# Resampling stage: x1 is added on TensorE, the bias in the last sum, and the first offsets of a window are made a step earlier

## What is computed

```
x1  = x  + dilation(groupnorm(x))                  # morphological dilation, 11 x 11 taps
out = x1 + deformable(groupnorm(x1))
# deformable(v): h = depthwise3x3(proj(v)); h = gelu(batchnorm(h))
#   offset = tanh(off_w @ h) * 1/255               # 2 channels: dy, dx for each pixel
#   bilinear sampling of v at (pixel + 0.5 + offset), zero outside the image
```

```
ph  = (tx + 1) * dh
f   = 0.5 * (tx + 1) * dd + dv
out = ph + (ty + 1) * f + scale * x1 + bias
```

## Time and profile before

| what | value |
|---|---|
| median of 3 runs | 11159.03 us (11152.15 to 11159.74) |
| the profiled execution: its time, its span | 11149.29 us, 11147.4 us |
| `resample`, first to last DVE instruction of its loop | from 10161.93 to 11143.07 us of the span |
| busy share of the whole span | DVE 95%, ACT 89%, POOL 82%, PE 75% |
| TensorE's granted clock, mean of the span | 0.922 |

### The profile page before, as it was taken

How to read it: one execution, slowest core, us unless ns; L and a number is a source line. 1 busy time by engine, 2 the same in 40 slices (tenths; PEclk the granted TensorE clock), 3 DMA queues, 4 the chain that set the end, 5 groups by cost and what they waited for, 6 DMA issues and landing times. The chain is left out here.

```text
span 11147.4 us, 74869 instructions
## 1 busy us (share of the span) xinstructions
PE 8347.9 (75%) x16532; PEld 3201.8 (29%) x16532; DVE 10631.9 (95%) x5882; ACT 9898.5 (89%) x7193; POOL 9104.7 (82%) x2891
## 2 busy tenths in 40 slices
PE   1777777777777777777777777777777777886665
PEld 0222222222222222222222222222222223332222
DVE  8999999999999999999999999999999998998999
ACT  2999999999999999999999999999999987776666
POOL 2888888888888888888888888888888885666777
PEclk9999999999999999999999999999999998998888
DMA  7666666666666666666666666666666663444555
GB/s 286 128 128 129 129 129 129 129 128 128 128 128 128 129 125 126 128 128 128 125 129 127 129 125 128 127 128 126 129 128 128 126 120 157 159 160 168 212 213 213
DMA packets 386979, 1573.30 MB, mean 141 GB/s; under 512 B 20944, under 2 KB 127568, under 8 KB 324432
## 3 DMA queue, kind: packets, MB, share of 16 engines
q0 software_dynamic: 218256, 901.04, 44.9%
q1 hardware_dynamic: 168256, 667.25, 16.0%
HBM read 465.90 MB, written 201.33 MB: 60 GB/s over the span
## 5 line engine op out<-in xcount | busy, mean ns | idle before, releaser
L446 POOL TENSOR_TENSOR m_pool<-r_pool,u 128x2048 f32<-128x2048 f32 x1536 | 6777.4, 4539 | 919.6 <-ACT r_pool L540 860.6
L495 PE MATMUL chain<-dx,mats 128*128 128x512 f32 x6144 | 3111.2, 649 | 952.9 <-ACT chain L558 951.9
L643 DVE SCALAR_TENSOR_TENSOR acc_a<-m_pool,kt,acc_a 128x2048 f32<-128x2048 f32 x1472 | 3465.7, 2354 | 60.2 <-POOL m_pool L446 17.7
L495 PE MATMUL chain<-dx,neg_ident 128*128 128x512 f32 x4608 | 2417.7, 672 | 851.0 <-ACT chain L558 850.6
L643 DVE SCALAR_TENSOR_TENSOR acc_a<-u,kt,acc_a 128x2048 f32<-128x2048 f32 x960 | 2261.2, 2355 | 31.9
L540 ACT ACTIVATE r_pool<-dx,gap_l 128x2048 f32<-128x2048 f32 x1024 | 2051.6, 2004 | 75.4 <-POOL m_pool L446 36.2
L495 PEld LDWEIGHTS chain<-dx,mats 128*128 128x128 f32 x6144 | 1167.2, 201 | 2896.7 <-ACT chain L558 1747.4
L643 DVE SCALAR_TENSOR_TENSOR acc_a<-t,kt,acc_a 128x2048 f32<-128x2048 f32 x768 | 1808.2, 2354 | 22.8
L558 ACT ACTIVATE chain<-chain,gap_r 128x1024 f32<-128x1024 f32 x1536 | 1631.0, 1089 | 110.6 <-PE chain L495 110.2
L495 PE MATMUL chain<-u,mats 128*128 128x512 f32 x3072 | 1457.9, 606 | 216.9 <-ACT chain L558 216.9
L495 PEld LDWEIGHTS chain<-dx,neg_ident 128*128 128x128 f32 x4608 | 919.5, 211 | 2348.8 <-ACT chain L558 1458.5
(11 more groups left out here) (144 smaller groups left out, 6976.5 us busy)
## 6 DMA issues: line engine op xcount, KB each, us to landing
t<-u POOLq DMA_DIRECT2D x768, 1059.0 KB, 8.7
u<-x_dram SPq DMA_DIRECT2D x28, 3328.0 KB, 27.5
xw<-x_scratch SPq DMA_DIRECT2D x64, 1152.0 KB, 6.9
hw<-h_scratch SPq DMA_DIRECT2D x66, 1024.0 KB, 8.9
x<-xc POOLq DMA_DIRECT2D x65, 1024.0 KB, 8.8
xt<-x_dram SPq DMA_DIRECT2D x32, 2048.0 KB, 14.4
xc<-x_dram SPq DMA_DIRECT2D x64, 1024.0 KB, 4.7
x_scratch<-x SPq DMA_DIRECT2D x64, 1024.0 KB, 9.8
```

The source lines that it names most:

```text
L446: nc.gpsimd.tensor_tensor(m_pool[j % MP][:], r_pool[j % RP][:], u[s][:, k * CR + di:k * CR + di + CR, base:base + W], ALU.add).then_inc(m_ ...
L495: added = nc.tensor.matmul(chain[h][:, r:r + 2, :], weight, src[:, top:top + 2, dj:dj + W], start=False, stop=True, skip_group_check=True)
L643: nc.vector.scalar_tensor_tensor(out=acc_a[:], in0=src, scalar=k_base, in1=acc_a[:], op0=ALU.subtract, op1=ALU.max).then_inc(a_done, 1)
```

## The change

DVE has five instructions for a part instead of six. The sum `res = ph + z` is gone, and ACT makes no `z`. In its place PE multiplies `xw` by a diagonal matrix `zdiag` that holds the scale of x1 (one for each group, made once ahead of the loop), and adds the product in PSUM onto `ph`, which DVE has written there (`add_z`, two matmuls for each part). The bias is the scalar operand (`tab[:, 5, ...]`) of the last instruction, `res = (ph + bias) + f`. For the accumulation PE opens `ph` once with two matmuls ahead of the loop.

The product `(ty + 1) * f` is written into `f` in SBUF rather than into `ty`, so that `ty` is free after this instruction (`w_ready`), and no longer only after the last sum. PE issues the offsets in another order: `tx` of the second part and of the next window's first part are issued ahead of that part's `ty`, and `ge` of the next window is waited for in the middle of a window. ACT takes the tanh of the next window's first `tx` ahead of `y`. POOL's `dh` waits for `f` of window n - 2 instead of its last sum. Each DVE instruction of a part now waits for the one before it. `xw` has four buffers instead of two, and x1 is loaded three windows ahead; SP's list is written out instead of looped. The computation of `dd` from columns of `dv` is as before.

```diff
@@ -1003,7 +1003,8 @@
-    channel_mean, same_image = mats[:, 2, :], mats[:, 3, :]
+    XS = 4
+    ident, channel_mean, same_image = mats[:, 0, :], mats[:, 2, :], mats[:, 3, :]
...
+        xw = [sb(f"xw{s}", [P, VR + 1, W]) for s in range(XS)]
-        z = [sb(f"z{s}", [P, VR, W]) for s in range(2)]
...
+        zdiag = sb("zdiag", [P, GROUPS, P])
...
+        F0, W0, OFFY0, D0, R0 = 3, 1, 2, 6, 1
...
+                for n in range(NALL):
+                    g, w = divmod(n, NV)
+                    if n > 0:
+
+                        sp.wait_ge(z_added, 2 * n)
+                    load_x(n + XS - 1)
+                    sp.wait_ge(ge_ready, n + 1)
+                    load_h(n + 2)
+                    sp.wait_ge(res_ready, R0 + 2 * n + 2)
+                    sp.dma_start(out_pl[g * P:(g + 1) * P, w * (VR * W):(w + 1) * (VR * W)],
+                                 res[n % 2][:].rearrange("p r w -> p (r w)")).then_inc(stored[n % 2], 16)
...
+                def offset_x(n, s, p):
+
+                    pe.wait_ge(f_ready, n * 2 + (p - 1 + F0))
+                    for r in range(0, PR, 2):
+                        last = nc.tensor.matmul(tx[p][:, r:r + 2, :], off[:, 1, :],
+                                                ge[s % 2][:, p * PR + r:p * PR + r + 2, :], start=True, stop=True)
+                    last.then_inc(off_x, 1)
+
+                def offset_y(n, s, p):
+
+                    pe.wait_ge(w_ready, n * 2 + (p + W0))
+                    for r in range(0, PR, 2):
+                        last = nc.tensor.matmul(ty[:, r:r + 2, :], off[:, 0, :],
+                                                ge[s % 2][:, p * PR + r:p * PR + r + 2, :], start=True, stop=True)
+                    last.then_inc(off_y, 1)
+
+                def add_z(n, g, s, p):
+
+                    pe.wait_ge(o_ready, n * 2 + (p + 1))
+                    for r in range(0, PR, 2):
+                        last = nc.tensor.matmul(ph[:, r:r + 2, :], zdiag[:, g, :],
+                                                xw[s % XS][:, p * PR + r:p * PR + r + 2, :],
+                                                start=False, stop=True, skip_group_check=True)
+                    last.then_inc(z_added, 1)
...
-                with nc.Fori(0, NALL // 2, engines=PE_ONLY) as i:
-                    for s in range(2):
-                        n = i * 2 + s
-                        pe.wait_ge(ge_ready, n + 1)
-                        for p in range(2):
-
-                            pe.wait_ge(part_x, n * 2 + (p + 1))
-                            for r in range(0, PR, 2):
-                                last = nc.tensor.matmul(tx[p][:, r:r + 2, :], off[:, 1, :],
-                                                        ge[s][:, p * PR + r:p * PR + r + 2, :],
-                                                        start=True, stop=True)
-                            last.then_inc(off_x, 1)
-                            pe.wait_ge(part_y, n * 2 + (p + 3))
-                            for r in range(0, PR, 2):
-                                last = nc.tensor.matmul(ty[:, r:r + 2, :], off[:, 0, :],
-                                                        ge[s][:, p * PR + r:p * PR + r + 2, :],
-                                                        start=True, stop=True)
-                            last.then_inc(off_y, 1)
+                pe.wait_ge(ge_ready, 1)
+
+                for r in range(0, PR, 2):
+                    opened = nc.tensor.matmul(ph[:, r:r + 2, :], ident, ge[0][:, r:r + 2, :],
+                                              start=True, stop=True, skip_group_check=True)
+                opened.then_inc(ph_open, 1)
+                offset_x(0, 0, 0)
+                offset_y(0, 0, 0)
+                for g in range(GROUPS):
+                    with nc.Fori(0, NV // XS, engines=PE_ONLY) as i:
+                        for s in range(XS):
+                            n = i * XS + (g * NV + s)
+                            offset_x(n, s, 1)
+                            add_z(n, g, s, 0)
+                            offset_y(n, s, 1)
+                            pe.wait_ge(ge_ready, n + 2)
+                            offset_x(n + 1, s + 1, 0)
+                            add_z(n, g, s, 1)
+                            offset_y(n + 1, s + 1, 0)
...
+                    act.wait_ge(xw_loaded[s % XS], loads * 16)
+                    act.wait_ge(diffs, n * 3 + (D0 - 3))
...
+                    act.wait_ge(off_y, n * 2 + (OFFY0 - 2))
+                    nc.scalar.activation(ge[s % 2][:], hw[s % 2][:], ACT.Gelu, bias=bn[:, 3:4], scale=bn[:, 2:3]) \
                         .then_inc(ge_ready, 1)
-
-                def make_z(n, s):
-                    act.wait_ge(part_y, n * 2 + 1)
-                    passed(act, act_turns)
-                    nc.scalar.activation(z[s][:], xw[s][:, 0:VR, :], ACT.Identity,
-                                         bias=tab[:, 5, bass.ds(n, 1)],
-                                         scale=tab[:, 4, bass.ds(n, 1)]).then_inc(z_ready, 1)
...
-                    act.wait_ge(off_y, n * 2 + (p + 1 + 4))
+                    act.wait_ge(off_y, n * 2 + (p + 1 + OFFY0))
...
+                act.wait_ge(hw_loaded[0], 16)
+                nc.scalar.activation(ge[0][:], hw[0][:], ACT.Gelu, bias=bn[:, 3:4], scale=bn[:, 2:3]) \
+                    .then_inc(ge_ready, 1)
                 make_y(1, 1, 1)
-                make_ge(0, 0, 1)
-                make_z(0, 0)
-                with nc.Fori(0, NALL // 2, engines=ACT_ONLY) as i:
-                    for s in range(2):
-                        n = i * 2 + s
-                        make_tanh_x(n, 0)
+                make_tanh_x(0, 0)
+                with nc.Fori(0, NALL // XS, engines=ACT_ONLY) as i:
+                    for s in range(XS):
+                        n = i * XS + s
                         make_tanh_y(n, 0)
                         make_tanh_x(n, 1)
-                        make_z(n + 1, 1 - s)
-                        make_ge(n + 1, 1 - s, i + (1 + s))
+                        make_ge(n + 1, s + 1, i * 2 + ((s + 1) // 2 + 1))
                         make_tanh_y(n, 1)
-                        make_y(n + 2, s, i + 2)
+                        make_tanh_x(n + 1, 0)
+                        make_y(n + 2, s + 2, i + ((s + 2) // XS + 1))
...
-                        pool.wait_ge(part_y, n * 2 + 1)
+
+                        pool.wait_ge(f_ready, n * 2 + (F0 - 2))
...
+                    link(nc.vector.tensor_scalar(zdiag[:, g, :], ident, tab[:, 4, lo:lo + 1], None, ALU.mult))
...
-                dve.sem_inc(part_x, 2)
-                dve.sem_inc(part_y, 3)
-                dve.sem_inc(off_y, 4)
+                dve.sem_inc(f_ready, F0)
+                dve.sem_inc(w_ready, W0)
+                dve.sem_inc(off_y, OFFY0)
+                dve.sem_inc(res_ready, R0)
                 nc.vector.memset(cm[:], 0.0).then_inc(tables_ready, 1)
+                dve.wait_ge(ph_open, 1)
...
-                            at = n * 8 + 4 * p
                             rows = slice(p * PR, (p + 1) * PR)
                             part = n * 2 + (p + 1)
                             if p == 0:
-                                dve.wait_ge(stored[s], i * 16 + 16)
-                                dve.wait_ge(z_ready, n + 1)
-                                dve.wait_ge(diffs, n * 3 + 9)
+                                dve.wait_ge(diffs, n * 3 + (D0 + 3))
                             dve.wait_ge(tanh_x, part)
+
+                            dve.wait_ge(res_ready, n * 2 + (p + R0))
                             nc.vector.scalar_tensor_tensor(out=ph[:], in0=tx[p][:], scalar=1.0, in1=dh[s][:, rows, :],
-                                                           op0=ALU.add, op1=ALU.mult).then_inc(chain, 1)
+                                                           op0=ALU.add, op1=ALU.mult).then_inc(o_ready, 1)
+                            dve.wait_ge(o_ready, part)
                             nc.vector.scalar_tensor_tensor(out=tx[p][:], in0=tx[p][:], scalar=1.0,
                                                            in1=dd[s][:, rows, :],
-                                                           op0=ALU.add, op1=ALU.mult).then_inc(chain, 1)
-                            dve.wait_ge(chain, at + 1)
-                            nc.vector.tensor_tensor(res[s][:, rows, :], ph[:], z[s][:, rows, :], ALU.add) \
-                                .then_inc(chain, 1)
-                            dve.wait_ge(chain, at + 2)
+                                                           op0=ALU.add, op1=ALU.mult).then_inc(x_scaled, 1)
+                            dve.wait_ge(x_scaled, part)
                             nc.vector.scalar_tensor_tensor(out=f[:], in0=tx[p][:], scalar=0.5,
                                                            in1=dv[s][:, rows, 0:W],
-                                                           op0=ALU.mult, op1=ALU.add).then_inc(part_x, 1)
```

(17 more changed lines are left out.)

77 lines of the change are left out of this document (32 added, 45 removed).

## The result

The changed kernel takes 11005.88 us, the median of 4 runs (11004.33 to 11008.32). The kernel before, timed beside it, takes 11159.39 us (4 runs, 11152.15 to 11160.56). The ratio is 0.9865, with a 95% interval of 0.9849 to 0.9881: 1.35% faster, 153.5 us. The forecast was 10995 us, with a range of 10972 to 11065 and, for its first case, of 10975 to 11010.

The account below looks back on a forecast made before the run. DVE's chain of dependent steps was taken to bound the last stage's loop: 64 x 12.76 = 816.6 us instead of 981.1, plus 0.6 for `zdiag`, so 163.9 less: 10995 us, range 10972 to 11065.

Parts of the forecast that it names:

- first case: In the last stage's loop DVE's chain bounds, as forecast: 10975 to 11010 us in all, chance 0.70.
- DVE's chain bounds: In the last stage's loop, five DVE instructions a part, each waiting for its predecessor, set the time; chance 0.70.
- The sum of the chain: DVE's start-to-start distances in the loop: 6.33 us a part, 12.76 a window with 0.10 added, 816.6 for 64 windows.
- the distance from the last sum to the next `ph`: On DVE, put at 1.31 us after a convolution step with like operands; bounds 1.25 and 1.32.
- The 0.10 us ahead of the last sum: In a window's first part, a sequencer row waiting ahead of DVE's last sum adds 0.10 us, as in the convolution.
- The clock: PE at full speed throughout the loop, its only gap some 1.0 us a part; rival of PE bounding, slower: chance 0.05.
- The slacks: Work beside DVE's chain stays hidden: `add_z` 0.9 us early, POOL idle 0.9 a window, DMA 254 GB/s, ACT near 68%.
- The prologue: Ahead of the loop, making `zdiag` adds two small DVE instructions, 2 x 0.29 = 0.6 us.
- What the profile was to show: Loop signs: DVE 96% or more, `ph` 12.7 to 12.8 us apart, PEclk 0.97 or more, no DVE wait for POOL.
- The total: Whole kernel: 981.1 - 816.6 - 0.6 = 163.9 us less, giving 10995 us on the median.

Follow-up runs that it names:

- a1_swap: Changed kernel with the two waits ahead of DVE's `ph` in the other order, the one for the last sum first; 10999.59 us.
- a2_static_bias: Changed kernel with DVE's loop run once per channel group, so the last sum's scalar has a fixed address and needs no register; 10997.14 us.
- a3_both: Changed kernel with both the edits of a1_swap and a2_static_bias; 10993.42 us, ratio to the kernel before 0.9853.
- a4_free_tx: Changed kernel without the wait of DVE's `tx` step for the `ph` step; 10993.67 us, ratio to the kernel before 0.9852.
- c2_all_small: Changed kernel with the edits of a1_swap, a2_static_bias and a4_free_tx together; 10971.08 us, ratio to the kernel before 0.9835.
- b5_ty_early_psum: Kernel before, with the product written to `f`, `ty` released right after it, and the sum with `z` kept in PSUM; 11096.38 us, ratio 0.9947.
- b3: Changed kernel with one more product with a weight of zeros in each `add_z` group on PE; 11001.26 us.
- b4: Changed kernel with two more products with a weight of zeros in each `add_z` group on PE; 11053.93 us.
- b1_ty_early: Kernel before, with the product written to `f`, `ty` released after it, and a last sum reading two SBUF tiles; 11211.75 us, ratio 1.0051.
- b2: Changed kernel with PE's offsets and ACT's first tanh in the old order, none a step ahead; 11005.06 us, ratio to the kernel before 0.9864.
- c1_interleaved: Changed kernel with DVE's steps interleaved over two parts, none waiting for its predecessor, and earlier loads; 10931.80 us, ratio to the kernel before 0.9798.

## Why the prediction was right

**DVE's chain bounds: right, and shown.** No wait for another engine stands in a window, and every edit of the chain came out in the loop at its size: 64 windows less 0.14, 0.12, 0.26, 0.27 and 0.53 us in a1_swap, a2_static_bias, a3_both, a4_free_tx and c2_all_small.

**The sum of the chain: 12.76 forecast, 13.00 measured.** The term that was too small is the distance from the last sum to the next `ph`, put at 1.31 us: it is 1.39, and 0.08 x 128 = 10 us of the loop are this. a1_swap shows the cause, the order of two waits. Another 0.02 us a window stand before the last sum (1.38 where 1.36 was counted). The rest is about 0.01 us in most steps: they were put at 1.25 or 1.26, the lower of the values in the earlier trace rows, and are 1.26 or 1.27. In all it is 0.24 x 64 = 15.4 us, the loop's 832.05 against 816.6. The durations were right: the last sum was to take about 1.28 us and takes 1.284.

**The 0.10 us ahead of the last sum: right in size, not in what it is.** It measures 0.12 (1.38 instead of 1.26 in first parts alone). The prediction put it down to a sequencer row that waits, after a step of another stage. a2_static_bias leaves the waits where they are and removes it: it is the register of the bias. That the two sizes are near each other was luck.

**The clock: right.** It was 1.00 throughout, with pauses of 1.02 and 1.14 us a part. That pauses of 1.3 us leave the clock alone was read from another stage and holds here. b5_ty_early_psum shows the other side, with a granted clock of 0.85 over 700 us of its loop. Here it is on PE in order of time: after 3.55 us of idleness four records take 2.46 us instead of 1.98. One window earlier, after 3.56 us, they take 3.78.

```profile
10564.07 2.46 PE L1120 MATMUL ty<-ge,off 128*128 128x512 f32 x4 [3.55 <-DVE f L1270]
```

**The slacks: right.** `add_z` 0.9 forecast, 1.1 measured, and tested from above by b3 and b4. POOL 0.9 forecast, 1.20 measured, more because the window is longer. DMA 254 GB/s forecast, 247 measured; 211 x 15.33 / 13.00 is 249. ACT 68% forecast, 65% measured.

**The prologue: twice what was forecast**, 1.2 us instead of 0.6. From the stage's first DVE instruction to the first `ph` it is 23.4 to 23.6 us in the three kernels with the old opening (before, b1, b5) and 24.59 or 24.60 in the changed kernel and the six variants of it that leave the opening alone (a1 to a4, b2, c2). The two `zdiag` take 0.28 and 0.29 us, as forecast, and with their gaps lengthen the chain of the tables by 0.35 us each. The rest is idle time ahead of DVE's last instruction before the loop, 0.84 us where it was 0.37; what it waits for there was not tested.

**What the profile was to show.** DVE was to be busy for 96% or more, and is for 95.2%. `ph` was to start 12.7 to 12.8 us apart, and starts 13.00 apart. The other signs came as stated: no releaser but DVE itself, PEclk 0.97 or more, PE idle about 1 us before `ty`, POOL idle before `dh`, released by `y`.

**The total.** The difference was forecast at 163.9 us. The loop fell 15.4 us short of it and the prologue 0.6, which leaves 147.9; the medians moved 153.5, and those 5.6 us are the spread of executions. They fell in the forecast's favour, by luck: the median is 11 us above the 10995, where the loop and the prologue account for 16.

Not settled: why the second of two waits costs about 0.07 us more than the first when it is the late one. The profile shows its row on the sequencer; what the first one saves was not measured.

## What to carry to other kernels

Where one engine's chain bounds, add up start-to-start distances, not durations, and look for what stands between two steps: a wait on the step just ahead, a second wait that is over last, a register in an address. Removing an instruction from such a chain gains less than its length if its neighbours did not wait for each other before and do now (0.7 of 1.13 us here), and moving an independent step between dependent ones gains without removing anything (c1_interleaved, 11.75 us a window, where c2_all_small has 12.47). Before a tile is moved from PSUM to SBUF, see whether the instruction that reads it then has both inputs in SBUF while GpSimd works.

## What the runs showed of the hardware

- Of two waits ahead of one DVE instruction, the one written second has a row of its own on the sequencer. If it is the late one, the instruction starts 1.39 us after its predecessor's start instead of 1.31 to 1.32 (a1_swap; the predecessor takes 1.28 us).
- A scalar operand whose address is worked out in a register right ahead of the instruction delayed it by 0.12 us: 1.38 against 1.26 us from start to start (a2_static_bias).
- A wait on the instruction just ahead costs 0.13 us: 1.27 against 1.14 us from start to start, for tiles of 128x1024 (a4_free_tx).
- A DVE sum with both inputs in SBUF took 3.44 us instead of 1.23 when it started 2.18 us into POOL's `dv`, and POOL's next instruction 4.46 us instead of 3.60 (b1_ty_early). With one input in PSUM neither happens in this stage's loop, in any other kernel here.
